# An attention-weighted factorization machine on one core: the head of the program rebuilt, rows of two fills gathered from the given table, gathers without a limit in flight, and five fills with late transposes

## The reference

```python
V = emb_v[x]                                   # x: (32, 2048) indices, after the wrap and clamp of a lookup
iu, ju = np.triu_indices(F, k=1)
VV = V[iu] * V[ju]                             # 496 pairs
hid = relu(einsum('pbk,kh->pbh', VV, at_w) + at_b)
score = einsum('pbh,ho->pbo', hid, at_h)
pooled = sum(VV * score, axis=0)
logit = pooled @ p + (w0 + sum(w1[x], axis=0))
return sigmoid(logit)
```

## Time and profile before

| | |
|---|---|
| median of 3 runs | 843.54 us (842.78 to 846.02) |
| span of the profiled execution, first to last instruction | 835.8 us |
| PE busy | 784.1 us, 94% of the span |
| DVE, ACT, POOL busy | 722.5, 640.7 and 555.4 us |
| rows moved by POOL's queue | 528 gathers, 16896 packets |

### The profile page before, as it was taken

How to read it: one execution, slowest core, us unless ns; L and a number is a source line. 1 busy time by engine, 2 the same in 40 slices (tenths; PEclk the granted TensorE clock), 3 DMA queues, 4 the chain that set the end, 5 groups by cost and what they waited for, 6 DMA issues and landing times.

```text
span 835.8 us, 26345 instructions
## 1 busy us (share of the span) xinstructions
PE 784.1 (94%) x10550; PEld 277.6 (33%) x10550; DVE 722.5 (86%) x1221; ACT 640.7 (77%) x674; POOL 555.4 (66%) x537
## 2 busy tenths in 40 slices
PE   0488996999999999999999999999999999999998
PEld 0123332333333333333333333333333333333332
DVE  4278897699999999999999999999999999999894
ACT  0267775788798887878878788898888888888785
POOL 5577777666677676666766766677667666766720
PEclk9989998999999999999999999999999999999999
DMA  7533268445423466544332347644434457633200
GB/s 257 99 25 24 26 22 25 23 22 22 23 22 23 20 22 23 21 22 24 21 22 22 23 21 22 23 24 21 22 21 23 21 22 23 24 22 22 11 1 1
DMA packets 19398, 24.27 MB, mean 29 GB/s; under 512 B 9960, under 2 KB 10029, under 8 KB 19373
## 3 DMA queue, kind: packets, MB, share of 16 engines
q0 software_dynamic: 16896, 17.07, 43.4%
q1 hardware_dynamic: 1535, 6.64, 2.1%
q10 hardware_dynamic: 942, 0.22, 0.1%
HBM read 20.59 MB, written 3.31 MB: 29 GB/s over the span
## 4 chain that ended last, share of the span: by engine, by line
PE 86%; DMA 5%; POOL 5%; issue 2%; ACT 1%; DVE 0%; ACTq 0%; POOLq 0%
PE Z L591 52%; PE SG L607 26%; POOL rows L303 5%; PE SG L621 4%; PE Z L553 4%; DMA rows<-table,joint_idx 3%; DMA rows<-in_L_rec_emb_v_dram,idx 2%; ACT pV L471 0%; ACT H L526 0%; DMA idx_raw<-in_r_x_dram 0%; PE Z L685 0%; ACT V L460 0%; PE Z L664 0%; ACT y_sb L537 0%; ACTq L247 0%
## 5 line engine op out<-in xcount | busy, mean ns | idle before, releaser
L303 POOL DMA_INDIRECT rows<-table,joint_idx x496 | 518.8, 1046 | 224.0 <-issue 139.7
L445 DVE TENSOR_TENSOR X<-V 128x992 f32<-128x992 f32 (+15 forms) x1024 | 635.6, 692 | 28.8 <-ACT V L500 14.8
L526 ACT ACTIVATE H<-Z,bias 128x1024 f32<-128x1024 f32 x512 | 529.7, 1121 | 113.2 <-PE Z L591 109.8
L591 PE MATMUL Z<-X,w_sb 64*64 64x512 f32 x4096 | 477.2, 600 | 7.4 <-DVE X L445 3.4
L591 PEld LDWEIGHTS Z<-X,w_sb 64*64 64x64 f32 x4096 | 147.0, 132 | 288.7 <-issue 283.2
L607 PE MATMUL SG<-H,score_w 128*32 128x512 f32 x2048 | 239.4, 597 | 0.0
L607 PEld LDWEIGHTS SG<-H,score_w 128*32 128x32 f32 x2048 | 56.8, 109 | 172.8 <-issue 96.0
L471 ACT ACTIVATE pV<-V,pmask 128x1024 f32<-128x1024 f32 x64 | 81.5, 1276 | 0.1
L413 DVE TENSOR_TENSOR prod<-SG,gram 128x512 f32<-128x512 f32 x32 | 22.1, 691 | 63.3 <-PE SG L607 63.3
L460 ACT COPY V<-Z 128x1024 f32<-128x1024 f32 x31 | 31.4, 1013 | 42.4 <-PE Z L553 42.4
L621 PEld LDWEIGHTS SG<-V,pV 128*32 128x32 f32 x4096 | 42.7, 109 | 23.9 <-issue 19.3
(11 more groups left out here) (46 smaller groups left out, 35.1 us busy)
## 6 DMA issues: line engine op xcount, KB each, us to landing
rows<-table,joint_idx POOLq DMA_INDIRECT x496, 3.7
table<-joined SPq DMA_DIRECT2D x4, 792.0 KB
H<-in_L_rec_emb_v_dram SPq DMA_DIRECT2D x4, 768.0 KB, 8.3
rows<-in_L_rec_emb_v_dram,idx POOLq DMA_INDIRECT x16, 5.3
w_all<-in_L_rec_w_dram,idx POOLq DMA_INDIRECT x16
idx_raw<-in_r_x_dram SPq DMA_DIRECT2D x2, 64.0 KB, 2.1
idx_raw<-in_r_x_dram ACTq DMA_DIRECT2D x2, 64.0 KB, 2.3
table<-tail SPq DMA_DIRECT2D x1, 54.7 KB
```

Source lines behind the costliest of these rows:

```text
L303: pool.indirect_dma_start(out=rows[t % 2][:, g * FILL_M + m, half, c0:c1], out_offset=None, in_=source, in_offset=bass.IndirectOffsetOnAxi ...
L445: last_one = nc.vector.tensor_tensor(xo, vj, vi.unsqueeze(3).to_broadcast(shape), ALU.mult)
L526: nc.scalar.activation(H[:, s % H_SLOTS, :, COLS * g:COLS * g + COLS], Z[:, z_slot(t, r), :, :], ACT.Relu, bias=bias[:, 0:1]).then_inc(hid ...
L591: done = nc.tensor.matmul(Z[64 * par:64 * par + 64, z_slot(t, r), half, :], w_sb[k, :], X[k, s % X_SLOTS, par, COLS * g:COLS * g + COLS], ...
```

## The change

Five things change, all in the head and in what follows from it:

1. The join of the table (two copies of w1, two of its tail, four of the pieces) moves from DVE to ACT, where it stands ahead of all relus.
2. `first_keep_v` moves from ACT to DVE, and DVE's constants that depend on loads (`pmask`, the head weights in `score_w`) move behind round 1 of fill 0.
3. `PLAIN_FILLS` is 2: fill 1 too gathers from the given table, without its w1, and POOL's end has 32 gathers of w1 in place of 16.
4. No gather waits for an earlier gather's landing.
5. `HEAD_FILLS` = 5 fills are written out, and fills 1 to 4 have their turn ahead of round 12. The loop begins at fill 5.

Cut to its core:

```diff
-LATE_FILLS = (1, 2)
+HEAD_FILLS = 5
+LATE_FILLS = range(1, HEAD_FILLS)
...
-PLAIN_FILLS = 1
+PLAIN_FILLS = 2
...
-LANES, IN_FLIGHT, HELD_FILLS = 4, 3, 4
...
-            fill(0, 0, True, False)
-            fill(1, 1, False, False)
-            fill(2, 0, False, False)
-            with eng.Fori(3, FILLS - 2, 2) as t:
+            for t in range(HEAD_FILLS):
+                fill(t, t % 2, t == 0, False)
+            with eng.Fori(HEAD_FILLS, FILLS - 2, 2) as t:
...
-                            if held and n >= IN_FLIGHT:
-                                pool.wait_ge(rows_landed[(n - IN_FLIGHT) % LANES], 16 * ((n - IN_FLIGHT) // LANES + 1))
...
-                            arrived = rows_landed[n % LANES] if held else rows_gathered[t % 2]
+                            arrived = rows_gathered[t % 2] if t else first_gathered[g]
...
             pool.wait_ge(idx_ready, 1)
             gather(0)
+            pool.wait_ge(idx_ready, 2)
+            gather(1)
             pool.wait_ge(idx_ready, 4)
             pool.wait_ge(table_stored, 16 * (PIECES + 1))
-            gather(1)
             pool.wait_ge(first_turned, 2)
             gather(2)
             for t in range(3, FILLS):
                 pool.wait_ge(rows_turned, t - 2)
-                pool.wait_ge(w1_kept, 2 * (t - 1 - PLAIN_FILLS))
+                if t - 2 >= PLAIN_FILLS:
+                    pool.wait_ge(w1_kept, 2 * (t - 1 - PLAIN_FILLS))
                 gather(t, paced=True)
...
-            dve.wait_ge(w1_loaded, 32)
-            for c in (0, 1 + EMB):
-                nc.vector.tensor_copy(joined[:, :, c], raw_w1[:, :]).then_inc(w1_joined, 1)
-                nc.vector.tensor_copy(tail[:, :, c], tail_w1[:, :]).then_inc(w1_joined, 1)
-            for k in range(PIECES):
-                dve.wait_ge(raw_loaded[k], 16)
-                r0, r1 = k * PIECE, (k + 1) * PIECE
-                nc.vector.tensor_copy(joined[:, r0:r1, 1:1 + EMB], raw[:, r0:r1, :]).then_inc(rows_joined[k], 1)
...
+            def first_keep_v(g):
+
+                dve.wait_ge(first_turned, g + 1)
+                nc.vector.tensor_copy(V[0][:, g * GROUP:(g + 1) * GROUP, :], SG[1][:, :, :]).then_inc(first_v, 1)
...
                     if first and r in (0, STEPS // 2):
+                        first_keep_v(g)
                         dve.wait_ge(first_v, g + 1)
+                    if first and r == 2:
+                        loaded_consts()
...
+            act.wait_ge(w1_loaded, 32)
+            for c in (0, 1 + EMB):
+                nc.scalar.copy(joined[:, :, c], raw_w1[:, :]).then_inc(w1_joined, 1)
+                nc.scalar.copy(tail[:, :, c], tail_w1[:, :]).then_inc(w1_joined, 1)
+            for k in range(PIECES):
+                act.wait_ge(raw_loaded[k], 16)
+                r0, r1 = k * PIECE, (k + 1) * PIECE
+                nc.scalar.copy(joined[:, r0:r1, 1:1 + EMB], raw[:, r0:r1, :]).then_inc(rows_joined[k], 1)
...
-                    keep_w1(1, 1)
...
-                for lane in range(LANES):
-                    pe.wait_ge(rows_landed[lane], landed(GATHERS // 2 * (g + 1)))
-                pe.nop(nofuse=True)
+                pe.wait_ge(first_gathered[g], 16 * GATHERS // 2)
...
-            products(1, 1, False, False)
-            products(2, 0, False, False)
-            products(3, 1, False, False, head)
-            with pe.Fori(3, FILLS - 2, 2) as t:
+            for t in range(1, HEAD_FILLS):
+                products(t, t % 2, False, False)
+            products(HEAD_FILLS, HEAD_FILLS % 2, False, False, head)
+            with pe.Fori(HEAD_FILLS, FILLS - 2, 2) as t:
```

More of the change, by code:

```diff
@@ L195, in afm_kernel @@
         w1_first = sem("w1_first")
-        rows_landed = [sem(f"rows_landed{lane}") for lane in range(LANES)]
+        first_gathered = [sem(f"first_gathered{g}") for g in range(2)]
         first_turned = sem("first_turned")
@@ L230, in gathered @@
         def gathered(t, parity):
-            return 16 * GATHERS // 2 * (t - parity - HELD_FILLS + 2)
-        def landed(gathers):
-            return 16 * gathers // LANES
+            return 16 * GATHERS // 2 * (t - (1 if parity else 2) + 2)
         def piece(dram, k):
@@ L286, in gather @@
             def gather(t, paced=False):
-                joint, held = t >= PLAIN_FILLS, t < HELD_FILLS
+                joint = t >= PLAIN_FILLS
                 source, at_rows = (flat, joint_idx) if joint else (emb_v, idx)
@@ L382, in _, with loaded_consts @@
             nc.vector.tensor_scalar(upper_first[:, :], upper[:, :], first_half[:, :], None, ALU.mult).then_inc(mask_chain, 1)
-            dve.wait_ge(mask_chain, 6)
-            dve.wait_ge(p_loaded, 32)
-            for half in range(2):
-                rng = slice(64 * half, 64 * half + 64)
-                last = nc.vector.tensor_copy(pmask[rng, half:half + 1], pcol[rng, :])
-            last.then_inc(pmask_ready, 1)
-            dve.wait_ge(score_w_cleared, 1)
-            dve.wait_ge(h_loaded, 32)
-            for half in range(2):
-                rng = slice(64 * half, 64 * half + 64)
-                own = slice(HALF_FIELDS * half, HALF_FIELDS * half + HALF_FIELDS)
-                last = nc.vector.tensor_scalar(score_w[rng, :, own], own_step[rng, :, own], hcol[rng, 0:1], None, ALU.mult)
-            last.then_inc(consts_ready, 1)
+            def loaded_consts():
+                dve.wait_ge(mask_chain, 6)
+                dve.wait_ge(p_loaded, 32)
+                for half in range(2):
+                    rng = slice(64 * half, 64 * half + 64)
+                    last = nc.vector.tensor_copy(pmask[rng, half:half + 1], pcol[rng, :])
+                last.then_inc(pmask_ready, 1)
+                dve.wait_ge(score_w_cleared, 1)
+                dve.wait_ge(h_loaded, 32)
+                for half in range(2):
+                    rng = slice(64 * half, 64 * half + 64)
+                    own = slice(HALF_FIELDS * half, HALF_FIELDS * half + HALF_FIELDS)
+                    last = nc.vector.tensor_scalar(score_w[rng, :, own], own_step[rng, :, own], hcol[rng, 0:1], None, ALU.mult)
+                last.then_inc(consts_ready, 1)
+            def first_keep_v(g):
+                dve.wait_ge(first_turned, g + 1)
+                nc.vector.tensor_copy(V[0][:, g * GROUP:(g + 1) * GROUP, :], SG[1][:, :, :]).then_inc(first_v, 1)
             def mask_gram(t, parity):
@@ L495, in _ @@
             nc.scalar.activation(warm[:, :], ident[0:QUARTERS, 0:1], ACT.Sigmoid).then_inc(sigmoid_loaded, 1)
-            def first_keep_v(g):
-                act.wait_ge(first_turned, g + 1)
-                nc.scalar.copy(V[0][:, g * GROUP:(g + 1) * GROUP, :], SG[1][:, :, :]).then_inc(first_v, 1)
-            first_keep_v(0)
+            act.wait_ge(w1_loaded, 32)
[6 more added lines that the diff above has]
+                nc.scalar.copy(joined[:, r0:r1, 1:1 + EMB], raw[:, r0:r1, :]).then_inc(rows_joined[k], 1)
             act.wait_ge(bias_loaded, 32)
@@ L542, in turn @@
             def turn(t, parity):
-                if isinstance(t, int) and t < HELD_FILLS:
-                    for lane in range(LANES):
-                        pe.wait_ge(rows_landed[lane], landed(GATHERS * (t + 1)))
-                    pe.nop(nofuse=True)
-                else:
-                    pe.wait_ge(rows_gathered[parity], gathered(t, parity))
+                pe.wait_ge(rows_gathered[parity], gathered(t, parity))
                 embs = rows[parity][:, :, :, :].rearrange("p t h k -> p t (h k)")
```

2 lines of the change are left out of this document (removed).

## The result

The changed kernel takes 846.88 us (median of 20 runs, 840.79 to 851.36), the kernel before 841.75 us in the same comparison (20 runs, 839.3 to 846.46): a ratio of 1.0054, 95% interval 1.0034 to 1.0074. It is slower by about half a per cent, where I had forecast 833.6 us with a range of 828 to 843. The profiled execution of the change has a span of 846.6 us and took 848.52 us, 1.9 us above its span. Over all executions on record of kernels near 840 us, the device time lies 1.8 to 2.2 us above the span. The profiled execution of before, with its span of 835.8 us, so took some 837.7 us and was a quick one; the 7.7 us that I had put down to what stands before the first and behind the last instruction are for the most part that luck. 10.8 us of difference between the spans stand against 5.1 us between the medians.

A forecast was written before the change was run, and what follows sets the result against it. TensorE's own work is 86% of the chain, so only its waits can be won. The span: - 4.9 (fill 0) - 6.0 (fills 1 to 6) + 1.0 (wait at fill 6) = - 9.9 us; median 843.5 - 9.9 = 833.6 us, range 828 to 843.

The forecast's parts named there:

- The pace of gathers: Gathers without a limit: the DMA side sets the pace, 1.47 us each, so a fill's rows take 23.5 us.
- the head: Fill 0: without the limit its second half's rows land at 35.0 us, 4.9 us earlier; range 31.1 to 38.5.
- the sixteenth at 35.0 us: Fill 0's last gather lands then: nine gathers beside loads and stores at 1.64 us, six at 1.47.
- the head gains nothing: Rival: stores hold fill 0's gathers back until 39 us or more, only late turns act; 838.5 us, chance 0.08.
- The rival of a head that gains more: Fill 0's gathers lose little beside loads and stores, the sixteenth lands at 31.1 us; 829.7 us, chance 0.13.
- The join on ScalarE: Table join in the head: starts at 14.75 us, copies 0.9 to 1.9 us, last store near 30 to 34, no cost.
- Fills 0 and 1: Rest of fill 0 unchanged, fill 1's rows just in time at 58.5 us, fill 1 starts at 64.6, 4.9 earlier.
- The stall of fill 3: Late turns remove the 6.74 us wait for fill 4's rows; fills 1 to 6 take 152.4 us, gaining 6.0.
- What is late next: Fill 6's rows, wanted ahead of round 6, land at 176.0 against 175.0: a 1 us wait, bounds 0 to 3.
- W1 of fill 1: Kernel's end: GpSimd's 32 gathers land by 826 us, linear term starts at 830.09; hidden by 4 us.
- The rival of the other side, the deep queue that costs more than the limit: Gathers pass at 1.64 us throughout, fill 6's rows come 17.4 us late; 851.5 us, chance 0.07.
- the 6 us: Gain forecast for fills 1 to 6 from late turns: 158.4 us before, 152.4 after.

The follow-up runs named there:

- e8: Kernel before with the join on ScalarE, V's first copy and the late constants on VectorE, on a slow chip: 1141.04 against 1143.13 us, ratio 1.0001.
- e3: Kernel before with the limit on gathers in flight taken out, nothing else: 847.6 us, ratio 1.0083.
- e1: Changed kernel with before's limit of three gathers in flight put back in fills 0 to 3: 840.43 us, ratio 0.9992.
- e10: Kernel before with five written-out fills, late turns in fills 1 to 4, limit of three in flight held for fills 0 to 5: 840.23 us, ratio 0.9979.
- e4: Kernel before with five written-out fills and late turns in fills 1 to 4, its limit held to fill 3: 842.67 us, ratio 1.0014.
- e5: Changed kernel with the limit of three in flight held for fills 0 to 5, on a slow chip: 1163.31 us, ratio 1.0226.
- e9: Changed kernel with the limit of three in flight held for fills 0 to 5, on a chip near 840 us: 841.07 us, ratio 0.9989.

## Why the prediction was wrong

**The pace of gathers** was right up to 35 us, and the step from it to **the head** was wrong. From 4 to 35 us the queue of the change served 506 gather packets, 15.8 gathers, just what "the sixteenth at 35.0 us" asks. But the sixteenth gather was complete only at 40.0, when 598 packets had passed: with many gathers open, packets of later ones go ahead of the last packets of an earlier one. (The records do not tell the gathers apart; this is the count of 598 against the 512 that sixteen gathers have, and a late semaphore would look the same.) Before, 519 packets had passed at 40 us, 16.2 gathers, with almost nothing open behind. I read packets served as gathers landed; with a deep queue this was 5 us off, and outside my bound of 38.5. The rival "the head gains nothing" gave the right time for the turn, though by another reason (stores that hold gathers back). The rule of the Trainium skill, SBUF — State Buffer, section on the "DVE blocks DMA" trap, was borne out by e8. The rival of a head that gains more had leaned on alternation between queues (the Trainium skill, DMA: Bandwidth & Descriptors, section on queues, rings and completion order). Whether packets alternate is not shown: 628 packets of the stores went beside 705 of the gathers in 40 us, but 95 beside 113 in 24 to 30 us and 250 beside 166 in 30 to 40. What is shown is that the stores did not go ahead of the gathers, and the head did not gain.

**The join on ScalarE**: its copies were priced well (1.40 us each, inside 0.9 to 1.9). "It can start at 14.75 us" was wrong by 3.9 us: w1's tail came later. The delay goes with the limit and not with the engine that joins (18.13 us in e3 and 18.62 in the change without it, 14.75, 15.23 and 15.11 in before, e1 and e8 with it). "The table's last store then lands some 4 us later than now, near 30 to 34 us" failed: 64.3. The estimate moved the stores by the start of their source and kept their speed, which they had only because the limit kept the gathers away; the wait of GpSimd and fill 1's loss follow from this step. "The join, its stores and V's copy on the other engine cost nothing" is the term put at nothing; with the stores beside the gathers it was fill 1's wait of 3.46 us and the lower clock behind it. Fill 2's first gather went out at 65.03 us where I had 47.

**Fills 0 and 1.** Fill 1 starts at 70.9 us where I had 64.6: 5.0 of it is the turn, the remainder a longer rest of fill 0 (30.8 us after the turn, 29.4 before). It then takes 32.3 in place of 27.1: 3.46 us of wait, and the clock after it, 0.89 in the window.

**The stall of fill 3**: right as far as it went. The turns that stand inside fills 2 to 4 wait for no DMA any more, and fills 2 and 3 take 24.9 and 26.2 against my 25.3 (together 0.5 us more). But its sum took fill 4 at 25.3, and it took 33.9. This is the largest single term, and it was counted nowhere: the packets of TensorE's instructions on q8, beside a deep queue of gathers. The earlier trace rows had 2% of "issue", which I did not ask about; the gap in fill 4 is 6.83 us, and the clock behind it costs most of the rest (TensorE is busy for 26.61 us there, 24.25 in fill 5).

**What is late next** was wrong in kind: fill 6 does not wait. Its rows were gathered behind the stall of fill 4, which gave them time; this reason is read from one trace.

**W1 of fill 1** was hidden: the linear term at 840.88 us follows TensorE's own work.

The sum: to the start of fill 7 I had 64.6 + 152.4 + 1.0 = 218.0 us; the trace has 237.4. Of these 19.4 us, 6.3 are fill 0, 5.2 fill 1, 0.5 fills 2 and 3, 8.6 fill 4, and - 1.2 fills 5 and 6 (24.6 and 24.6 against 24.1 and 26.3). The last 1.3 us, to a span of 846.6 against 825.9, come later. The median was off by less, 13.3 us, since the 7.7 us that I added to the span were 0.3 here. The rival of the other side, the deep queue that costs more than the limit, had the right sign and a time 4.6 us too high (851.5), but a wrong mechanism: I let the gathers themselves get slower, and it was their neighbours that did. Its chance, 0.07, was too low, since only the gathers' own pace had been asked of it.

How much the late turns bring alone stays inside what is measurable: e10, where neither stall is left in fills 1 to 4, is 0.2% faster, with an interval that takes in no change. Whether another depth or length of the limit would keep the 6 us was tried only on the slow chips, and is open.

## What to carry over

A limit on transfers in flight is judged by all users of the DMA engines: list the stores and the instruction fetches that run in its stretch, and ask when each must be served. Count the loads that feed the first step among them. Packets served at a steady pace don't say when a certain transfer is complete; in this head, with a deep queue, it completed 5 us later than its share. An "issue" gap of microseconds in the middle of a written-out stretch is to be held against the start of the instruction queue's last packet ahead of its end. And packets of one program are compared by their number in the queue, not by their time.

## What was not expected of the hardware

- How long a gather packet stands on an engine changed with the depth of GpSimd's queue: 79.0% of 16 engines' time for 569 packets against 26.6% for 539, at the same traffic.
- TensorE's instructions come in 16 KB packets of some 0.95 us, and TensorE went on 2.2 to 2.5 us after such a packet had started, 24 times out of 24 (160.1 after 157.8 in e4, 164.33 after 161.9 in the change).
- Chips differ: the same kernel before took 840 to 842 us in three comparisons and 1113 to 1143 us in the three others. On such a chip TensorE stood in "issue" before matmuls of Z for 86.9 us in all (e5), against 1.2 us for the same kernel on the other (e9).
